# A message-passing layer on Trainium2: the normalised rows h in the second gather buffer and 13 further rows, the residual in pieces of three tiles

## The chip, the cores and the metric

The kernel runs on one core of one Trainium2 chip. The metric is the device time of one execution in microseconds (us), the median of several runs. Five engines work side by side, each through its own list of instructions in order: PE (TensorE, matmuls), DVE (VectorE), ACT (ScalarE), POOL (GpSimd), and SP (SyncE), which here only issues DMA transfers. They meet at semaphores: an instruction that waits for one holds everything behind it on its own engine.

## The reference

There are 6250 nodes with 96 features, and 206250 directed edges sorted by destination, each with 96 attributes.

```python
h = jnp.maximum(_layernorm(x, axis=-1), 0.0)
m = h[src] + edge_attr
aggr = jax.ops.segment_sum(m, dst, num_segments=6250)
hidden = jax.nn.relu(aggr @ W1 + b1)              # 96 -> 192
out = x + (1.0 + eps[0]) * h + hidden @ W2 + b2    # 192 -> 96
```

## The kernel before

**Blocks.** The nodes are cut into 49 blocks (NT) of 128. For 45 of them (NM) the sum of `h[src]` is made without a gather: DVE builds one-hot matrices of the sources' high and low parts (`z`, `lo_hot`, in four chunks a block, function `chunk`), PE multiplies them into counts of sources per destination (`octet`), ACT moves the counts to `adj`, and PE multiplies `adj` with h held in two fp16 parts (`sum_slots`). The edge attributes of a block are summed on PE by one-hots of the destinations (`sum_edges`, 72 matmuls).

**Gathered blocks.** The last four blocks (45 to 48, called gathered block 0 to 3) take the other way: SP loads their edge attributes, sources and destinations (`load_gathered`, 12 transfers), and POOL adds the rows h[src] onto the attributes in place with indirect DMAs from a copy of h in DRAM, 36 gathers of 128 rows for each block (line 524). Their sums are attached to the ordinary blocks 14, 24, 34 and 42 (ATTACHED). Two buffers are used in turn; each has GROUPS * GT = 36 rows of 96 values per partition, 72 rows together in `gather_home`. `gathered_buffer(j)` names the buffer of gathered block j.

**What else lies in these buffers.** At the start the raw `dst` and `src` lists (D and S) lie in the first and the second buffer. After that h itself (`h_sb`, 49 rows per partition) lies in `gather_home`: in all 36 rows of the first buffer and 13 of the second. h is read until the residual x + (1 + eps) h has been made in `x_sb` (function `residual`, line 734), which DVE does in pieces at the end of blocks 2 and later; `res_ready` counts them. Piece 0 is the 13 tiles 36 to 48, which frees the second buffer; six pieces of six tiles follow. So gathered block 0 goes into the second buffer, gathered block 1 into the first.

**Keys.** The packed (destination, source) keys of two blocks at a time come as a window from DRAM, fetched by POOL with an indirect DMA (`fetch`, line 486) that stands between the gathers in POOL's list: one fetch for every 23/3 gathers (FETCH_EVERY, FETCH_PER). Window 8 stands ahead of gather 31 (counted from 0 over all gathered blocks), window 9 ahead of gather 39, window 10 ahead of gather 46. Ahead of gather 36, the first of gathered block 1, POOL waits once for `gather_in` of that block's buffer (line 515), that is for its loads. Gathers are also held back to a pace of 13 per 3 blocks by `edges_done` (line 523). DVE takes window q in block 2(q - 1), between its first and second chunk (`pick`, line 676); PE and ACT then turn the keys for blocks 2q and 2q + 1.

**Order on DVE in a block b:** chunk 0; `pick` in even blocks; chunk 1; the one-hots of block b + 1's edges (`edge_hots`, which waits for that block's `dst` load, line 762); in blocks 14, 24, 34, 42 the one-hots of a gathered block; the output addition of block b - 4 (`finish`); the join of block b - 2's two partial sums (`next_join`, line 792); chunks 2 and 3; a residual piece. **On PE:** eight octets with the previous block's slots between them; after octet 2 come the turn of the joined sums (line 1090), the edge sum (line 1079) and the small layers.

**Order on SP.** For b from 3: wait for the edge sum of block b - 3 (`edges_done` at b - 2), then the eight loads of block b. Behind block 5's loads it issues gathered block 0's, behind block 12's those of gathered block 1, behind blocks 18 and 28 the other two (they wait for the sum that frees the buffer). Then the store of block b - 7.

Of the kernel before, what the change touches and what calls it, by code (L numbers as in the profile page):

```python
# [12 lines left out]
P = 128  # L13
# [8 lines left out]
GROUPS = P // GROUP  # L22
GT = 9
SPLIT = 100
TURN = 3
# [11 lines left out]
ATTACHED = (14, 24, 34, 42)  # L37
# [8 lines left out]
DEVIATION_AT = (15, 24)  # L46
RES_FIRST = 36
RES_ROWS = 6


def build(nc, x, src, dst, edge, w1, b1, w2, b2, eps, out):
    N, C = x.shape
    E = src.shape[0]
    H = w1.shape[1] // C
    NT = -(-N // P)
    NM = NT - GATHERED
# [4 lines left out]
    MPAIRS = -(-NM // 2)  # L61
    GE = P * GT
    ELAST = E - GE
    GCOLS = PAIRS * 2 * GROUPS
# [21 lines left out]
    with ExitStack() as ctx:  # L86
        def sb(name, shape, dt=F32):
            return ctx.enter_context(nc.sbuf_tensor(name, shape, dt))
# [16 lines left out]
        dst_sb = [sb(f"dst{k}", [P, GROUPS, GT], I32) for k in range(TURN)]  # L105
        gather_home = sb("gathered_edges", [P, 2, GROUPS, GT, C])
        gathered = [gather_home[:, k, :, :, :] for k in range(2)]
        gather_dst = [sb(f"gather_dst{k}", [P, GROUPS, GT], I32) for k in range(2)]
# [14 lines left out]

        h_sb = gather_home[:, :, :, :, :].rearrange("p k g t c -> p (k g t c)")[:, 0:NT * C].rearrange("p (t c) -> p t c", c=C)
        packed_lo = adj_home[:, :, :, :].rearrange("p k h n -> p (k h n)")[:, 0:4 * DW].rearrange("p (e four) -> p e four", four=4)[:, :, 2:4]
# [97 lines left out]
        words_ready = sem("words_ready")  # L223
# [101 lines left out]
        THIRDS = [slice(0, 16), slice(16, 32), slice(32, NT)]  # L325
        RES = [(RES_FIRST, NT)] + [(t, t + RES_ROWS) for t in range(0, RES_FIRST, RES_ROWS)]

# [12 lines left out]
        def gathered_buffer(j):  # L340
            return (j + 1) % 2

# [6 lines left out]
        def _(sp):  # L349
# [56 lines left out]
            for b in range(TURN, NM):  # L406
                sp.wait_ge(edges_done, b - TURN + 1)
                load(b)
                if b == TURN + 2:
                    sp.wait_ge(h_stored, 32)  # L410
                    sp.wait_ge(res_ready, 1)
                    load_gathered(0)
                if b == TURN + 2 + len(RES):
                    sp.wait_ge(res_ready, len(RES))
                    load_gathered(1)
                if attached(b - TURN - 1) is not None and attached(b - TURN - 1) + 2 < GATHERED:
                    j = attached(b - TURN - 1)
                    sp.wait_ge(gather_summed, j + 1)
                    load_gathered(j + 2)
                if b >= STORE_LAG:  # L420
                    store(b - STORE_LAG)
                if attached(b - STORE_LAG) is not None:
                    store_gathered(attached(b - STORE_LAG))
# [145 lines left out]
        def _(v):  # L569
# [206 lines left out]
            def finish(b):  # L776
                v.wait_ge(out_done, b + 1)
                if b < RES_FIRST:
                    v.wait_ge(res_ready, 2 + b // RES_ROWS)
                if b >= OBS:  # L780
                    v.wait_ge(out_stored[b % OBS], 16 * (b // OBS))
                nc.vector.tensor_tensor(ob[b % OBS][:, :], x_sb[:, b, :], mlp_ps[:, OUT_AT:OUT_AT + C], ALU.add).then_inc(out_ready, 1)  # L782
# [17 lines left out]
            def finish_gathered(j):  # L800
                v.wait_ge(gather_out_done, j + 1)
                if j >= 1:
                    v.wait_ge(gather_stored, 16 * j)
                nc.vector.tensor_tensor(gather_ob[:, :], x_sb[:, NM + j, :], mlp_ps[:, GATHERED_OUT_AT:GATHERED_OUT_AT + C], ALU.add).then_inc(gather_out_ready, 1)
# [473 lines left out]
```

## Time and profile before

| | before |
|---|---|
| median of 3 runs | 525.16 us (523.21 to 527.09) |
| the profiled execution | 525.82 us |
| its span, first to last instruction | 523.9 us |
| mean granted TensorE clock | 0.997 of full |
| PE, matmuls | 469.9 us (90%) |
| PEld, weight loads beside them | 446.9 us (85%) |
| DVE | 482.8 us (92%) |
| ACT | 414.3 us (79%) |
| POOL | 299.4 us (57%) |
| DMA | 110.03 MB, mean 210 GB/s |

The span is the traced part; the profiled execution's own time is 1.9 us longer. A share near 100% says that an engine is rarely idle, not that it decides the end at that moment: in stages the deciding engine differs, so the rows further down are taken by stretch and by queue. An "idle before" in square brackets is what the engine waited for just ahead of the instruction.

### The profile page before, as it was taken

The page shows a single profiled execution, that of the slowest core. Times are in us where ns is not written, and L with a number is a line of the kernel's source. Part 1 is how long each engine was busy: PE and PEld are TensorE (multiplying, and loading weights), DVE is VectorE, ACT ScalarE, POOL GpSimd, SP SyncE. Part 2 cuts the span into 40 slices and gives each one's busy share as a digit, 9 for nine tenths or more (in the row PEclk, how much of TensorE's full clock was granted, in tenths as well). Part 3 has the DMA queues.
Part 4 walks back from the last instruction along what each step waited for, and adds up shares of the span by engine and source line. Part 5 has one row for each costly group of instructions (what it writes and reads, how often), then busy time and mean ns, then how long its engine had stood idle before and what let it go on. Part 6 is the DMA issues. An engine that isn't in the chain of part 4 may idle for free.

```text
span 523.9 us, 22551 instructions
## 1 busy us (share of the span) xinstructions
PE 469.9 (90%) x9174; PEld 446.9 (85%) x9174; DVE 482.8 (92%) x727; ACT 414.3 (79%) x637; POOL 299.4 (57%) x188
## 2 busy tenths in 40 slices
PE   0525789999999999999999999999999999999994
PEld 0414688999899899999999999999999999998994
DVE  7998999999999999989999998899999999999870
ACT  0798777788888887888888788888888888886861
POOL 1330000788888888687888888888888881000000
PEclk9999999999999999999999999999999999999998
DMA  6769888998889987999998789999888887765000
GB/s 204 246 210 251 248 239 243 265 251 225 210 218 237 293 228 177 259 239 277 220 231 212 181 219 254 276 246 229 209 221 191 212 216 187 201 194 148 6 9 21
DMA packets 96867, 110.03 MB, mean 210 GB/s; under 512 B 68900, under 2 KB 70552, under 8 KB 96630
## 3 DMA queue, kind: packets, MB, share of 16 engines
q1 hardware_dynamic: 74854, 98.39, 63.1%
q0 software_dynamic: 21904, 10.13, 15.2%
q8 instruction: 75, 1.23, 0.9%
q14 instruction: 34, 0.28, 0.2%
HBM read 102.00 MB, written 6.48 MB: 207 GB/s over the span
## 4 chain that ended last, share of the span: by engine, by line
PE 77%; DVE 8%; SPq 6%; issue 4%; ACT 3%; DMA 1%; DVEq 0%; ACTq 0%
PE agg_ps L1085 31%; PE oct_ps L1073 22%; PE agg_ps L1079 14%; PE key_ps L1097 5%; PE mlp_ps L1102 4%; SPq L374 3%; DVE lo_hot L595 2%; ACT adj L917 2%; DVE z L595 1%; SPq L375 1%; SPq L373 1%; PE key_ps L1090 1%; DVE hot L602 1%; DMA gathered_edges<-in_dst 1%; ACT hid L930 1%
## 5 line engine op out<-in xcount | busy, mean ns | idle before, releaser
L917 ACT ACTIVATE adj<-oct_ps 128x784 f16<-128x784 f32 x360 | 299.5, 865 | 74.8 <-PE oct_ps L1073 70.6
L524 POOL DMA_INDIRECT gathered_edges<-h_rows,gather_src x144 | 264.5, 1837 | 48.6 <-issue 41.8
L1085 PE MATMUL agg_ps<-hl,adj 128*128 128x192 f16 x2205 | 232.9, 246 | 0.6 <-issue 0.3
L595 DVE TENSOR_TENSOR lo_hot<-iota_z,key 128x2048 f16<-128x2048 f16 x180 | 219.0, 1217 | 0.0
L1073 PE MATMUL oct_ps<-z,lo_hot 128*128 128x98 f16 x2880 | 190.7, 209 | 15.6 <-DVE lo_hot L595 7.8
L1073 PEld LDWEIGHTS oct_ps<-z,lo_hot 128*128 128x128 f16 x2880 | 164.3, 99 | 19.1 <-issue 8.2
L1085 PEld LDWEIGHTS agg_ps<-hl,adj 128*128 128x128 f16 x2205 | 173.5, 97 | 3.1 <-ACT adj L917 0.7
L595 DVE TENSOR_TENSOR z<-z_marks,key 128x1568 f16<-128x1568 f16 x180 | 173.9, 966 | 0.4 <-PE oct_ps L1073 0.4
L1079 PE MATMUL agg_ps<-edges,hot 128*32 128x96 f32 x3240 | 77.5, 250 | 2.3 <-DVE hot L748 2.3
L1079 PEld LDWEIGHTS agg_ps<-edges,hot 128*32 128x32 f32 x3240 | 68.0, 111 | 7.7 <-DVE hot L748 2.6
L486 POOL DMA_INDIRECT win<-packed_keys,row_i x23 | 26.8, 1166 | 68.4 <-DMA gathered_edges<-in_edge_attr 61.8
L980 ACT ACTIVATE hot<-hot 128x1152 f32<-128x1152 f16 x44 | 51.4, 1168 | 5.4 <-DVE hot L595 3.7
L595 DVE TENSOR_TENSOR hot<-iota_z,rel 128x1152 f16<-128x1152 f16 x44 | 33.3, 758 | 1.5
L1097 PE MATMUL key_ps<-aggT,w_sb 96*96 96x128 f32 x180 | 30.0, 288 | 2.4 <-issue 1.1
L930 ACT ACTIVATE hid<-key_ps,b_sb 96x128 f32<-96x128 f32 x90 | 27.3, 356 | 2.2 <-PE mlp_ps L1102 1.5
L1097 PEld LDWEIGHTS key_ps<-aggT,w_sb 96*96 96x96 f32 x180 | 21.0, 162 | 9.0 <-ACT key L905 3.2
L792 DVE TENSOR_REDUCE agg<-agg_ps 128x96 f32<-128x192 f32 x45 | 15.9, 353 | 12.9 <-PE agg_ps L1085 12.8
L1102 PE MATMUL mlp_ps<-w_sb,hid 97*128 97x96 f32 (+1 forms) x180 | 26.5, 269 | 0.7 <-ACT hid L930 0.7
L1102 PEld LDWEIGHTS mlp_ps<-w_sb,hid 97*128 97x128 f32 (+1 forms) x180 | 23.6, 191 | 0.9 <-ACT hid L930 0.9
L953 ACT ACTIVATE gathered_edges<-x_sb,shift,rstd 128x96 f32<-128x96 f32 x49 | 17.9, 452 | 0.5 <-DVE shift L619 0.5
L782 DVE TENSOR_TENSOR ob<-x_sb,mlp_ps 128x96 f32<-128x96 f32 x45 | 11.1, 247 | 6.9 <-PE mlp_ps L1102 6.9
L1090 PE MATMUL key_ps<-ident,agg 128*96 128x128 f32 x45 | 12.6, 280 | 5.3 <-DVE agg L792 3.9
(145 smaller groups left out, 186.3 us busy)
## 6 DMA issues: line engine op xcount, KB each, us to landing
edges<-in_edge_attr SPq DMA_DIRECT2D x180, 432.0 KB
gathered_edges<-in_edge_attr SPq DMA_DIRECT2D x16, 432.0 KB
dst<-in_dst SPq DMA_DIRECT2D x180, 4.5 KB
gathered_edges<-h_rows,gather_src POOLq DMA_INDIRECT x144
out<-ob SPq DMA_DIRECT2D x45, 48.0 KB
packed_keys<-adj SPq DMA_DIRECT2D x1, 1632.0 KB, 6.0
h_rows<-gathered_edges SPq DMA_DIRECT2D x1, 1200.0 KB, 9.2
h_rows<-gathered_edges SPq DMA_DIRECT2D x1, 1152.0 KB, 8.4
```

The source lines that it names most:

```text
L486: nc.gpsimd.indirect_dma_start(out=to[:, :, :].rearrange("p e two -> p (e two)"), out_offset=None, in_=keys_dram, in_offset=bass.IndirectO ...
L524: nc.gpsimd.indirect_dma_start(out=gathered[k][:, g, t, :], out_offset=None, in_=h_dram, in_offset=bass.IndirectOffsetOnAxis(ap=gather_src ...
L595: return nc.vector.tensor_tensor(out.rearrange("p t (w two) -> p t w two", two=2), marks[0:out.shape[0], 0:width].rearrange("p (o w two) - ...
L917: return nc.scalar.activation(adj[k][:, :, 2 * OCT * o:2 * OCT * (o + 1)].rearrange("p h (t q) -> p t h q", q=2), oct_ps[:, o % 2, :].rear ...
L930: last = nc.scalar.activation(to[0:C, j, :], key_ps[0:C, at + P * j:at + P * (j + 1)], ACT.Relu, bias=b1_sb[:, j:j + 1])
L953: last = nc.scalar.activation(h_sb[:, t, :], x_sb[:, t, :], ACT.Relu, bias=shift[:, t:t + 1], scale=rstd[:, t:t + 1])
L980: nc.scalar.activation(hot[b % 2][:, :, :], hot16[:, :, :], ACT.Copy).then_inc(hot_ready, 1)
L1073: last = nc.tensor.matmul(oct_ps[:, o % 2, P * t:P * t + ZW], lo_hot[o // 2][:, at, :], z[o // 2][:, at, :], start=True, stop=True)
L1079: last = nc.tensor.matmul(sums[GROUP * g:GROUP * (g + 1), :], hots[:, g * GT + t, :], rows[:, g, t, :], start=fresh and t == 0, stop=False ...
L1085: last = nc.tensor.matmul(agg_ps[buf][:, 0:2 * C], adj[buf][:, h, :], hl[:, h, :], start=False, stop=(h == NT - 1), skip_group_check=True)
L1097: last = nc.tensor.matmul(key_ps[0:C, at + P * j:at + P * (j + 1)], w1_sb[:, j, :], turned_sums[:, :], start=True, stop=True)
L1102: last = nc.tensor.matmul(mlp_ps[:, at:at + C], hidden_values[0:C + 1 - j, j, :], w2_sb[0:C + 1 - j, j, :], start=(j == 0), stop=(j == H - 1))
```

## The change

h moves to the second buffer and 13 rows appended behind it: `gather_home` grows from 72 to 85 rows (4992 bytes per partition more). Gathered blocks 0 and 2 now use the first buffer, 1 and 3 the second. Gathered block 0's load no longer waits for a residual piece or the stored h, only for the key words and steps made from D. The residual is cut into pieces of three tiles: twelve for tiles 0 to 35, which share the second buffer, then one for the four gathered tiles 45 to 48, then three for tiles 36 to 44. These are 16 pieces at the ends of blocks 2 to 17 (the change's one-line summary says 17). Gathered block 1's load is issued behind block 17's loads (5 + 12) and waits for the first twelve pieces. The output additions wait for their piece.

```diff
--- before.py
+++ after.py
@@ -44,8 +44,7 @@
 STORE_LAG = 7
 KEYS_AFTER = 24
 DEVIATION_AT = (15, 24)
-RES_FIRST = 36
-RES_ROWS = 6
+RES_ROWS = 3
 
 
 def build(nc, x, src, dst, edge, w1, b1, w2, b2, eps, out):
@@ -60,6 +59,8 @@
     PAIRS = -(-NT // 2)
     MPAIRS = -(-NM // 2)
     GE = P * GT
+    GATHER_ROWS = GROUPS * GT
+    assert NT >= GATHER_ROWS and GATHER_ROWS % RES_ROWS == 0
     ELAST = E - GE
     GCOLS = PAIRS * 2 * GROUPS
     SPLITS = GCOLS // SPLIT
@@ -103,8 +104,8 @@
         edge_home = sb("edges", [P, TURN, GROUPS, GT, C])
         edges = [edge_home[:, k, :, :, :] for k in range(TURN)]
         dst_sb = [sb(f"dst{k}", [P, GROUPS, GT], I32) for k in range(TURN)]
-        gather_home = sb("gathered_edges", [P, 2, GROUPS, GT, C])
-        gathered = [gather_home[:, k, :, :, :] for k in range(2)]
+        gather_home = sb("gathered_edges", [P, GATHER_ROWS + NT, C])
+        gathered = [gather_home[:, GATHER_ROWS * k:GATHER_ROWS * (k + 1), :].rearrange("p (g t) c -> p g t c", t=GT) for k in range(2)]
         gather_dst = [sb(f"gather_dst{k}", [P, GROUPS, GT], I32) for k in range(2)]
         gather_src = [sb(f"gather_src{k}", [P, GROUPS, GT], I32) for k in range(2)]
         z_home = sb("z", [P, CHUNKS, CHUNK, ZW], F16)
@@ -121,7 +122,7 @@
         keyT = [sb(f"keyT{k}", [P, P], F16) for k in range(2)]
         win_lo = [win[k][:, :, :].rearrange("p e two -> p (e two)").bitcast(F16).rearrange("p (e four) -> p e four", four=4)[:, :, 2] for k in range(WINS)]
 
-        h_sb = gather_home[:, :, :, :, :].rearrange("p k g t c -> p (k g t c)")[:, 0:NT * C].rearrange("p (t c) -> p t c", c=C)
+        h_sb = gather_home[:, GATHER_ROWS:GATHER_ROWS + NT, :]
         packed_lo = adj_home[:, :, :, :].rearrange("p k h n -> p (k h n)")[:, 0:4 * DW].rearrange("p (e four) -> p e four", four=4)[:, :, 2:4]
         packed = adj_home[:, :, :, :].rearrange("p k h n -> p (k h n)").bitcast(I32)[:, 0:2 * DW].rearrange("p (e two) -> p e two", two=2)
         scratch = [gathered[k].rearrange("p g t c -> p (g t c)").bitcast(I32) for k in range(2)]
@@ -323,7 +324,9 @@
 
         ROWS = [slice(0, HALF), slice(HALF, NT)]
         THIRDS = [slice(0, 16), slice(16, 32), slice(32, NT)]
-        RES = [(RES_FIRST, NT)] + [(t, t + RES_ROWS) for t in range(0, RES_FIRST, RES_ROWS)]
+        RES_SHARED = GATHER_ROWS // RES_ROWS
+        RES = [(t, t + RES_ROWS) for t in range(0, GATHER_ROWS, RES_ROWS)] + [(NM, NT)] + [(t, min(t + RES_ROWS, NM)) for t in range(GATHER_ROWS, NM, RES_ROWS)]
+        assert 2 + RES_SHARED < ATTACHED[0] + 3
 
         def all_stored(engine):
 
@@ -338,7 +341,7 @@
             return ATTACHED.index(b) if b in ATTACHED else None
 
         def gathered_buffer(j):
-            return (j + 1) % 2
+            return j % 2
 
         def edge_rows(b):
             return edges[b % TURN]
@@ -407,11 +410,12 @@
                 sp.wait_ge(edges_done, b - TURN + 1)
                 load(b)
                 if b == TURN + 2:
+                    sp.wait_ge(words_ready, 1)
+                    sp.wait_ge(steps_ready, 1)
+                    load_gathered(0)
+                if b == TURN + 2 + RES_SHARED:
                     sp.wait_ge(h_stored, 32)
-                    sp.wait_ge(res_ready, 1)
-                    load_gathered(0)
-                if b == TURN + 2 + len(RES):
-                    sp.wait_ge(res_ready, len(RES))
+                    sp.wait_ge(res_ready, RES_SHARED)
                     load_gathered(1)
                 if attached(b - TURN - 1) is not None and attached(b - TURN - 1) + 2 < GATHERED:
                     j = attached(b - TURN - 1)
@@ -775,8 +779,7 @@
 
             def finish(b):
                 v.wait_ge(out_done, b + 1)
-                if b < RES_FIRST:
-                    v.wait_ge(res_ready, 2 + b // RES_ROWS)
+                v.wait_ge(res_ready, b // RES_ROWS + (1 if b < GATHER_ROWS else 2))
                 if b >= OBS:
                     v.wait_ge(out_stored[b % OBS], 16 * (b // OBS))
                 nc.vector.tensor_tensor(ob[b % OBS][:, :], x_sb[:, b, :], mlp_ps[:, OUT_AT:OUT_AT + C], ALU.add).then_inc(out_ready, 1)
@@ -799,6 +802,7 @@
 
             def finish_gathered(j):
                 v.wait_ge(gather_out_done, j + 1)
+                v.wait_ge(res_ready, RES_SHARED + 1)
                 if j >= 1:
                     v.wait_ge(gather_stored, 16 * j)
                 nc.vector.tensor_tensor(gather_ob[:, :], x_sb[:, NM + j, :], mlp_ps[:, GATHERED_OUT_AT:GATHERED_OUT_AT + C], ALU.add).then_inc(gather_out_ready, 1)
```

## Rows read from the trace of the kernel before

**Rows 1.** Busy time in three stretches: PE, PEld, DVE, ACT, POOL, clock, DMA share, GB/s.
```profile
95.00:115.00 20.00, 19.64 (x384) 18.56 (x382) 19.93 (x27) 16.38 (x25) 17.26 (x10) 1.00 0.97 270
...
255.00:295.00 40.00, 39.82 (x793) 38.47 (x790) 39.36 (x53) 34.39 (x51) 34.21 (x20) 1.00 0.87 221
...
521.00:524.00 3.00, 0.00 (x0) 0.00 (x0) 0.00 (x0) 0.00 (x0) 0.00 (x0) 0.50 0.03 6
```
**Rows 2.** Chain of waits, the edge sums on PE: start us, us, piece.
```profile
101.15 1.62 PE agg_ps L1079 x72
...
193.90 3.11 PE agg_ps L1079 x144
...
215.87 1.62 PE agg_ps L1079 x72
...
226.21 1.62 PE agg_ps L1079 x72
...
236.07 1.62 PE agg_ps L1079 x72
```
**Rows 3.** DVE in order of time: start us, us, line, operation [idle before <-releaser].
```profile
27.76 0.28 DVE L676 TENSOR_SCALAR keyT<-win,base 128x128 f16<-128x128 int32 x1
...
99.31 0.23 DVE L762 TENSOR_TENSOR rel<-dst,gbase 128x72 f16<-128x72 int32 x1
...
171.48 0.23 DVE L762 TENSOR_TENSOR rel<-dst,gbase 128x72 f16<-128x72 int32 x1 [2.26 <-DMA dst<-in_dst]
...
190.58 0.22 DVE L762 TENSOR_TENSOR rel<-dst,gbase 128x72 f16<-128x72 int32 x1
...
193.18 0.35 DVE L792 TENSOR_REDUCE agg<-agg_ps 128x96 f32<-128x192 f32 x1
...
209.26 0.28 DVE L676 TENSOR_SCALAR keyT<-win,base 128x128 f16<-128x128 int32 x1
...
213.60 0.36 DVE L792 TENSOR_REDUCE agg<-agg_ps 128x96 f32<-128x192 f32 x1 [0.94 <-PE agg_ps L1085]
```
**Rows 4.** SP's DMA issues in order of time: start us, us, line.
```profile
74.64 0.34 SPq L374 DMA_DIRECT2D dst<-in_dst  x1
...
88.33 0.33 SPq L383 DMA_DIRECT2D gathered_edges<-in_edge_attr  x1
...
95.61 0.33 SPq L374 DMA_DIRECT2D dst<-in_dst  x1
...
167.75 0.33 SPq L374 DMA_DIRECT2D dst<-in_dst  x1
...
197.75 0.33 SPq L374 DMA_DIRECT2D dst<-in_dst  x1
```
**Rows 5.** POOL in order of time, key steps, window fetches, first gather of block 1.
```profile
17.04 2.90 POOL L496 TENSOR_TENSOR lo_hot<-gathered_edges 127x1632 int32<-127x1632 int32 x1 [13.95 <-DVE adj L643]
...
25.06 1.00 POOL L486 DMA_INDIRECT win<-packed_keys,row_i  x1 [0.30 <-issue]
...
93.21 1.09 POOL L486 DMA_INDIRECT win<-packed_keys,row_i  x1 [61.79 <-DMA gathered_edges<-in_edge_attr]
...
177.56 1.72 POOL L524 DMA_INDIRECT gathered_edges<-h_rows,gather_src  x1 [0.30 <-issue]
...
183.69 1.59 POOL L486 DMA_INDIRECT win<-packed_keys,row_i  x1 [0.31 <-issue]
...
201.31 1.18 POOL L486 DMA_INDIRECT win<-packed_keys,row_i  x1 [0.30 <-issue]
```
**Rows 6.** The residual line: durations in ns (min/median/max), start of first and last.
```profile
L734 DVE SCALAR_TENSOR_TENSOR x_sb<-gathered_edges,eps_sb,x_sb x7: 808/809/1509, 73.4 to 135.6; 128x576 f32<-128x576 f32 x6, 128x1248 f32<-128x1248 f32 x1
```
**Rows 7.** PE in order of time, before and after its clock rose.
```profile
40.53 3.11 PE L1079 MATMUL agg_ps<-edges,hot 128*32 128x96 f32 x72 [2.33 <-DVE hot L748]
...
47.78 1.49 PE L1073 MATMUL oct_ps<-z,lo_hot 128*128 128x98 f16 x16 [4.14 <-ACT key L905]
...
53.30 0.52 PE L1073 MATMUL oct_ps<-z,lo_hot 128*128 128x98 f16 x8
```

## Prediction

> **What bounds the kernel now.** I read the stretches first, then the chain of waits, then the queues of DVE, SP and POOL one after the other. In the stretch 95 to 115 us DVE is busy 19.93 of 20 us and PE 19.64; from 255 to 295 us PE is busy 39.82 of 40 us and DVE 39.36 [rows 1]. So DVE sets the pace early and PE sets it later, and neither has room: a stop of either goes nearly whole into the end. The chain gives the pace. Each block has one sum of its edges (72 matmuls); those of blocks 17 and 18 start 9.86 us apart, which is PE's own period, while blocks 5 to 14 take (193.90 - 101.15) / 9 = 10.31 us each [rows 2]. In DVE's rows the thing to see is where it stands: 2.26 us before the edge numbers of block 13, because a transfer was late, and nowhere at those of block 6 [rows 3]. SP's rows give how long it takes to issue one block's loads and one gathered block's; POOL's rows give the gathers, and between them the window fetches [rows 4, 5]. The last are what the argument hangs on. A window holds the packed keys of two blocks; DVE needs window q in block 2(q - 1), in order, ahead of its second chunk. Window 9 is fetched at 183.69 us and used at 209.26 us [rows 3, 5], so today it has 25 us to spare.
>
> **The change, part by part.** *h moves, buffer order swaps.* Gathered block 0 goes into the buffer that h has left; its load is still issued behind block 5's, where SP follows block 5's loads without a pause, and the first window fetch behind it waits for these very edges [rows 4, 5]. The two new waits there are for the key words and for the steps made from them, over at 17.04 + 2.90 = 19.9 us [rows 5]; the old one, the first residual piece, ended at 75 us and did not hold SP either [rows 6]: nothing gained or lost. The 13 further rows cost space, not time.
>
> *Residual.* A piece of 576 elements takes 0.809 us and one of 1248 takes 1.509 [rows 6]; that is 0.208 us plus 1.04 ns an element, so a piece of three tiles takes 0.51 and the one of four 0.61. Six and one pieces (6.36 us) become sixteen (8.24 us; the lines give 16, whatever the summary counts). Nine more instructions thus cost DVE 1.9 us in all. The Trainium skill, page "VectorE: DVE Perf Modes", section on the TRN2 errata, speaks against such a cut: a fixed cost is paid per instruction, so many small tiles pay it many times; the about 150 cycles that it gives would make this 1.4 us and the sum 0.5 us less. Where it falls matters more. Block 2 saves 1.0 us, blocks 3 and 4 save 0.3 each, but DVE then comes to block 6's edge numbers 1.6 us before 99.31. SP issues the last of these at 95.61 and is busy without a pause until then, so it can't be earlier; the one row that did wait for such a load started 171.48 - 167.75 = 3.7 us after its issue [rows 3, 4]. 95.61 + 3.7 = 99.3: I take the whole 1.6 us as given back (ends: all kept, all lost). From there blocks 5 to 8 save 4 x 0.30 = 1.2, blocks 9 to 13 pay 5 x 0.51 = 2.55, and the 2.26 us before block 13's numbers goes, because the twelve loads of gathered block 1 no longer stand ahead of them on SP. Sum: DVE is 0.9 us earlier at block 14. PE's own pace would bring it there at 101.15 + 9 x 9.86 = 189.9, before 193.0, so DVE still decides and the 0.9 us is real. The ends are -2.5 (the 1.6 kept) and +1.35 (the 2.26 stays).
>
> *The waits of the output additions* are on counts that DVE itself raised at least two blocks before, in its own order: nothing.
>
> *Gathered block 1's load, five blocks later.* This is the term that decides. SP now issues it behind block 17's loads, and these wait for the edge sum of block 14, which ended at 193.90 + 3.11 = 197.0 and will end at 196.1. Behind SP's wait nothing is late by itself: the store of block 10 goes out later by the issue of twelve loads, and its buffer is asked for four blocks on. But POOL waits for this load before gather 36, and behind that wait in POOL's order stand gathers 36 to 38 and then the fetch of window 9. Today POOL starts gather 36 at 177.56 without a stop. Step by step:
> - SP starts block 17's loads 0.75 us after the sum, at 196.85 (197.75 today) [rows 4].
> - Block 5's loads and the gathered load behind them took from 74.64 to the last edges' issue at 88.33, 13.7 us [rows 4]. So the last edges go out at 210.5.
> - POOL went on 93.21 - 88.33 = 4.88 us after that issue [rows 4, 5]: 215.4.
> - Three gathers took 183.69 - 177.56 = 6.13 us [rows 5]: window 9 is fetched at 221.5.
> - No view shows when a window lands. From below: the first one was used 27.76 - 25.06 = 2.70 us after its fetch began, with idle queues [rows 3, 5]. From above: the 4.88 us of the loaded queue. Block 18's loads and the next gathered load will be in the queues, so I take the loaded end: 226.4.
> - DVE stands at window 9 from about 209.4 (209.26 - 0.9 + two pieces of 0.51) to 226.4, 17 us.
>
> The Trainium skill, page "DMA: Bandwidth & Descriptors", section "Anatomy of one DMA", gives about 2.0 us plus size over 436 GB/s for a transfer issued from GpSimd; for a window of 128 KB this is an estimate of 2.3 us, and the sum by it would be 2.6 us less.
>
> *What of this reaches the end.* From the window to the point where DVE joins block 14's sums it takes 213.60 - 0.94 - 209.26 = 3.40 us without waiting, and PE starts the edge sum 193.90 - 193.18 = 0.72 us after a join begins [rows 2, 3]. So block 16's edge sum starts at 226.4 + 4.1 = 230.5 in place of 215.87: 14.6 us later. DVE's usual lead covers only the difference of 17 and 14.6. While DVE stands PE has nothing for some 14 us. Its clock then falls: with no matmul from 521 us on the granted clock is 0.50, the lower of the two levels, 1.2 GHz [rows 1], and before 53 us, after idle stretches, 72 edge matmuls took 3.11 us against 1.62 later [rows 2, 7]. Dense work began at 47.78 and the first rows at full rate are at 53.30 [rows 7], 5.5 us. About 1.8 us of this passes while PE waits for the join anyway; half of the other 3.7 is lost: 1.85 us (ends 0 and 2.75). After that PE runs on at its old periods (10.34 for block 17 [rows 2]) and DVE, which managed 10.31 with a 0.81 us piece in each block, keeps up. Gathered block 1 is then complete in time: ten gathers and a fetch took 201.31 - 177.56 = 23.75 us [rows 5], so 36 take 86 and end at 301, and block 24 asks for them at 226.21 + 7 x 9.86 + 16 = 311.
>
> **The sum:** -0.9 is inside the start of the chain; +14.6 + 1.85 = +16.5 us. The profiled execution took 525.82 us, so 542.3; that execution is 0.66 us above the median of the runs, so 541.7.
>
> **The rivals.** *The fetch is not held: not slower.* POOL would pass the wait before gather 36 in time and the window would land before about 213, when PE would first miss the chunk behind it. Then only the 0.9 to 2.5 us remain as gain: 525.16 - 0.9 = 524.3. It decides at the fetch: it would have to go out by 208, 13 us before the time worked out. Against it stands the order of SP's and POOL's instructions, and SP's 13.7 us behind a sum that ends at 196. For it: only that I misread which count POOL waits for.
>
> *A second stop at window 10.* From window 9's fetch to window 10's POOL needs 201.31 - 183.69 = 17.6 us [rows 5], and DVE comes to the second pick two blocks later, at least 19.7 us. If the gathers are slowed further by two gathered loads in neighbouring blocks, the 2 us of margin goes and each further us is lost whole, as DVE then has no lead; two or three us late give about 544.5. For it: gathered block 2's load follows one block behind. Against it: the 17.6 us were themselves measured under full queues.
>
> *A shorter stop.* If the load lands as fast as SP issues, the window in 2.7 us and the clock stays up, each of these at its low end: 14.6 - 1.6 - 2.2 = 10.8 us, 536.0.
>
> **How the numbers follow.** Forecast 0.86, second stop 0.05, shorter stop 0.05, not held 0.04. Terms at the low ends together give 536, at the high ends (late start +2.2, window and issue +1.5, clock +0.9) 546.3; they will hardly all meet, and the second stop lies inside: 536 to 546, widened by 0.5 below for the spread of runs. A difference under 1% can't be told from none here (the three runs span 0.7%); 1% is 530.4. Only the unheld fetch ends below that, inside 1%; a gain of over 1% would need the unheld fetch and more than the 2.5 us: 0.01.
>
> **What would show it.** DVE: one idle stretch of about 17 us before the key row of window 9 (line of the key transposition's input), put down to a transfer; no 2.26 us before block 13's numbers. POOL: idle from about 177 to 215 before gather 36. PE: some 14 us without work before block 16's edge sum, and a granted clock of 0.50 in it and shortly after. Edge sums of blocks 5 to 8 closer than 10.2 us apart, and blocks 18 on 9.86 apart. It is wrong if POOL's fetch of window 9 goes out before 208, or if DVE's stop is there but PE's is much shorter.

## The result, and the profile after

The changed kernel takes 546.61 us, median of 4 runs (545.26 to 548.5), against 526.12 us of the kernel before in the same comparison (4 runs, 523.21 to 529.8): a ratio of 1.0395, 95% interval 1.0357 to 1.0434. Medians and ratios here and below leave out executions over 1.5% above the fastest of the same kernel; there is one, 549.92 us, in the run called again. The profiled execution took 548.5 us, its span is 546.6 us and its mean granted clock 0.970 (before: 525.82, 523.9 and 0.997). The forecast, slower, named the main mechanism, but it was 4.9 us short, and the upper end of the range, 546.0, was 0.6 us too low.

From the page of the kernel after, the granted clock and DVE in 40 slices of 13.7 us; before, the clock had a 9 in every slice:

```profile
DVE  7997999899999957099999999999999989999970
PEclk9999999999999969669999999999999999999998
```

The holes lie in slices 15 to 18 (191 to 246 us). The stretches of the kernel after, columns as in [rows 1]:

```profile
95.00:115.00 20.00, 18.60 (x372) 17.71 (x371) 18.56 (x26) 15.67 (x23) 17.56 (x9) 1.00 0.92 246
197.00:204.00 7.00, 6.62 (x150) 6.37 (x151) 1.71 (x2) 1.16 (x1) 0.00 (x0) 0.55 0.01 2
218.00:232.00 14.00, 3.45 (x52) 2.99 (x49) 0.00 (x0) 3.67 (x5) 7.27 (x6) 0.70 0.87 245
255.00:295.00 40.00, 39.60 (x787) 38.17 (x785) 38.87 (x51) 34.11 (x51) 34.21 (x20) 1.00 0.88 212
```

The two middle stretches in the kernel before:

```profile
197.00:204.00 7.00, 7.00 (x105) 6.91 (x105) 6.75 (x10) 5.39 (x9) 5.78 (x4) 1.00 0.77 180
218.00:232.00 14.00, 14.00 (x259) 13.69 (x258) 13.27 (x18) 11.50 (x18) 11.86 (x8) 1.00 0.90 220
```

There are two holes, not one. From 218 to 232 us DVE does nothing: that one was forecast. From 197 to 204 PE is busy, but at a granted clock of 0.55, nearly all of it at the lower level, 1.2 GHz: that one was not. The edge sums in the chain of waits of the kernel after, as in [rows 2]:

```profile
101.12 1.62 PE agg_ps L1083 x72
...
180.93 1.67 PE agg_ps L1083 x72
197.38 6.02 PE agg_ps L1083 x144
...
237.47 3.04 PE agg_ps L1083 x72
...
249.24 1.62 PE agg_ps L1083 x72
259.11 1.62 PE agg_ps L1083 x72
```

Block 5 is where it was, blocks 5 to 13 are (180.93 - 101.12) / 8 = 9.98 us apart (10.24 before, where block 13's sum starts at 183.07), and the sum of block 14 comes 3.5 us later than before and takes 6.02 us in place of 3.11. The sum of block 17, at 249.24, is 23.0 us behind the 226.21 of [rows 2]; from there the period is 9.87 (9.86 before), and the execution ends 22.7 us later. PE's rows at the two holes, in order of time:

```profile
197.38 3.11 PE L1083 MATMUL agg_ps<-gathered_edges,hot 128*32 128x96 f32 x72 [4.89 <-DMA gathered_edges<-h_rows,gather_src]
200.24 3.13 PE L1083 MATMUL agg_ps<-edges,hot 128*32 128x96 f32 x72
...
235.66 0.83 PE L1077 MATMUL oct_ps<-z,lo_hot 128*128 128x98 f16 x8 [14.07 <-DVE lo_hot L599]
```

Before the first, PE waited 4.89 us for gathers of gathered block 0; before the second, 14.07 us for DVE. DVE's rows (those of [rows 3], lines moved by 3 or 4) show why:

```profile
189.19 0.21 DVE L766 TENSOR_TENSOR rel<-dst,gbase 128x72 f16<-128x72 int32 x1
...
191.77 0.35 DVE L795 TENSOR_REDUCE agg<-agg_ps 128x96 f32<-128x192 f32 x1
...
233.29 0.28 DVE L680 TENSOR_SCALAR keyT<-win,base 128x128 f16<-128x128 int32 x1 [17.16 <-DMA win<-packed_keys,row_i]
```

One stop of 17.16 us at window 9. SP's rows of block 17's first issue and of the last gathered edges, to set beside [rows 4]:

```profile
204.11 0.33 SPq L377 DMA_DIRECT2D dst<-in_dst  x1
...
218.96 0.33 SPq L386 DMA_DIRECT2D gathered_edges<-in_edge_attr  x1
```

And POOL's rows, as in [rows 5]:

```profile
94.12 4.62 POOL L490 DMA_INDIRECT win<-packed_keys,row_i  x1 [62.73 <-DMA gathered_edges<-in_edge_attr]
...
116.58 3.77 POOL L490 DMA_INDIRECT win<-packed_keys,row_i  x1 [0.30 <-issue]
...
127.76 3.21 POOL L528 DMA_INDIRECT gathered_edges<-h_rows,gather_src  x1 [0.30 <-issue]
...
156.48 3.77 POOL L490 DMA_INDIRECT win<-packed_keys,row_i  x1 [0.30 <-issue]
...
176.44 4.31 POOL L528 DMA_INDIRECT gathered_edges<-h_rows,gather_src  x1 [0.30 <-issue]
...
187.62 3.19 POOL L528 DMA_INDIRECT gathered_edges<-h_rows,gather_src  x1 [0.30 <-issue]
...
193.41 2.14 POOL L528 DMA_INDIRECT gathered_edges<-h_rows,gather_src  x1 [0.30 <-issue]
223.21 1.54 POOL L528 DMA_INDIRECT gathered_edges<-h_rows,gather_src  x1 [27.65 <-DMA gathered_edges<-in_edge_attr]
...
228.76 1.00 POOL L490 DMA_INDIRECT win<-packed_keys,row_i  x1 [0.30 <-issue]
```

Two things are to be seen. Gather 36 starts at 223.21 behind a wait of 27.65 us, and window 9 is fetched at 228.76 (183.69 in [rows 5]). And six rows ahead of these, three gathers and three fetches, take 3.19 to 4.62 us; in the kernel before no gather took over 2.44 and no fetch between 93 and 202 us over 1.59. So gathered block 0, which starts 0.9 us later than before, has its last gather begun only at 193.41, where before gather 36 was already out at 177.56. From the first fetch to the end of gather 35 it took 101.4 us in place of 84.1 for the same 41 rows. At the 1.75 us that a row took before, the six long rows make 12.4 us of these 17.4, the other 35 the rest.

The residual came out as worked out:

```profile
L738 DVE SCALAR_TENSOR_TENSOR x_sb<-gathered_edges,eps_sb,x_sb x16: 506/508/608, 73.6 to 251.3; 128x288 f32<-128x288 f32 x15, 128x384 f32<-128x384 f32 x1
```

### The profile page after: what moved, and what is told of

The parts are those of the page before. It is cut to its first block, busy times and chain, and to the rows that moved or that the text cites. A ratio compares the mean times of both kernels' runs of the same rounds, so it can differ in the third digit from the quotient of the medians.

```text
span 546.6 us, 22562 instructions
## 1 busy us (share of the span) xinstructions
PE 474.7 (87%) x9174; PEld 451.9 (83%) x9174; DVE 484.6 (89%) x736; ACT 414.1 (76%) x637; POOL 317.3 (58%) x188
## 4 chain that ended last, share of the span: by engine, by line
PE 75%; SPq 8%; DVE 4%; issue 4%; DMA 4%; POOL 3%; ACT 1%; DVEq 0%; ACTq 0%
PE agg_ps L1089 30%; PE oct_ps L1077 21%; PE agg_ps L1083 14%; PE key_ps L1101 5%; PE mlp_ps L1106 4%; SPq L377 3%; POOL gathered_edges L528 3%; SPq L376 2%; SPq L378 2%; PE key_ps L1094 1%; DVE hot L606 1%; ACT adj L921 1%; DVE lo_hot L599 1%; DMA win<-packed_keys,row_i 1%; DMA gathered_edges<-in_dst 1%
## 5 line engine op out<-in xcount | busy, mean ns | idle before, releaser
L528 POOL DMA_INDIRECT gathered_edges<-h_rows,gather_src x144 | 272.4, 1892 | 71.2 <-issue 42.7
L1083 PE MATMUL agg_ps<-edges,hot 128*32 128x96 f32 x3240 | 80.4, 255 | 2.3 <-DVE hot L752 2.3
L1083 PEld LDWEIGHTS agg_ps<-edges,hot 128*32 128x32 f32 x3240 | 70.7, 114 | 7.8 <-DVE hot L752 2.6
L490 POOL DMA_INDIRECT win<-packed_keys,row_i x23 | 36.8, 1601 | 69.3 <-DMA gathered_edges<-in_edge_attr 62.7
L795 DVE TENSOR_REDUCE agg<-agg_ps 128x96 f32<-128x192 f32 x45 | 16.0, 354 | 13.8 <-PE agg_ps L1089 13.7
L680 DVE TENSOR_SCALAR keyT<-win,base 128x128 f16<-128x128 int32 x23 | 7.4, 324 | 17.2 <-DMA win<-packed_keys,row_i 17.2
L1094 PE MATMUL key_ps<-ident,agg 128*96 128x128 f32 x45 | 12.9, 286 | 5.2 <-DVE agg L795 3.6
```

The costliest lines, as they stand in the source:

```text
L490: nc.gpsimd.indirect_dma_start(out=to[:, :, :].rearrange("p e two -> p (e two)"), out_offset=None, in_=keys_dram, in_offset=bass.IndirectO ...
L528: nc.gpsimd.indirect_dma_start(out=gathered[k][:, g, t, :], out_offset=None, in_=h_dram, in_offset=bass.IndirectOffsetOnAxis(ap=gather_src ...
L1083: last = nc.tensor.matmul(sums[GROUP * g:GROUP * (g + 1), :], hots[:, g * GT + t, :], rows[:, g, t, :], start=fresh and t == 0, stop=False ...
L1094: return nc.tensor.transpose(key_ps[0:C, TURN_AT:TURN_AT + P], agg[:, :], ident[:, :])
```

## The experiments

Two questions. **First:** is the loss the late load of gathered block 1 (it holds POOL, POOL holds the fetch, the fetch holds DVE), and not the extra pieces, the moved h or the swapped buffers? **Second:** what made the six rows long, and is it what put the result above the forecast? Rivals there: the short pieces themselves, the new place of h, or the place in DVE's order at which a POOL row starts.

**The load late, by itself.** In the kernel before:

```diff
-                if b == TURN + 2 + len(RES):
+                if b == TURN + 2 + 12:
```

> The kernel before, with one edit: gathered block 1's load is issued behind block 17's loads, not behind block 12's. Layout, buffer order and the pieces of six tiles stay. Theory 1 (the late load holds POOL and with it window 9): DVE stands 15 to 18 us for window 9, PE some 14, and as POOL's rows of gathered block 0 stay short, PE waits for nothing in block 14: edge sum 14 ends near 196, time 538 to 543, ratio 1.025 to 1.032. Rival (what costs is the new place of h or the new buffer order, not the load's time): no stop at window 9, within 1% of before.

541.03 us, ratio 1.025 (1.019 to 1.0311), with seven old pieces, h in its old place and the buffers unswapped. DVE's stop and PE's wait are there (the views of waits and of POOL in order of time):

```profile
DVE keyT L676 <- DMA win<-packed_keys,row_i: 18.2, 1, 18.2
```
```profile
216.80 1.54 POOL L524 DMA_INDIRECT gathered_edges<-h_rows,gather_src  x1 [38.75 <-DMA gathered_edges<-in_edge_attr]
```

PE stood 14.7 us, and its next edge sum took 3.04 us. No POOL row was long (over 2.7 us), and PE did not wait in block 14. This one line gives most of the loss.

**All but the late load and the short pieces.** In the kernel after, pieces of six tiles; the load then follows block 11, since it is tied to their number:

```diff
-RES_ROWS = 3
+RES_ROWS = 6
```

> The changed kernel with pieces of six tiles: nine pieces, and since the shared rows are then free after six, gathered block 1's load goes out behind block 11's loads. New layout and new buffer order stay. Theory 1: no stop at window 9, time within 1% of before (521 to 528). If the long POOL rows come from DVE's shorter piece of 0.51 us (theory 1a), none over 2.6 us in gathered block 0 and gather 35 starts near 175 to 178. If they come from the new place of the buffers (theory 1b), there are again some of 3 to 4.6 us, gather 35 starts later than 188, PE waits some us in block 14, and the time is 528 to 533.

525.79 us, ratio 0.9986 (0.9954 to 1.0017): no difference, and no stop. Moving h and swapping the buffers cost nothing that can be measured. With RES_ROWS = 4 the load goes out behind block 14:

> The changed kernel with pieces of four tiles: 13 pieces, gathered block 1's load behind block 14's loads. By the chain measured in the changed kernel (30.0 us from the edge sum that the load waits for to window 9 in place) window 9 is there near 203 to 205 us, DVE asks for it near 209: no stop, so theory 1 says within 1% of before (522 to 529), unless long POOL rows come with a piece of 0.61 us too; then gather 35 starts later than 185 and PE waits up to 5 us in block 14 (528 to 534). The rival, that any load later than block 12's costs, says 529 or more without a wait in block 14.

526.31 us, ratio 1.0014 (0.9978 to 1.0049). There was no stop at window 9 either, though its trace has four long rows and PE waited 3.3 us in block 14, where the sum then took 4.88 us in place of 3.11. The traced execution took 531.19 us; it is one of three at 530.2 to 531.3, while the other seven took 524.3 to 527.3. That is what such a wait would cost, 3.3 + 1.8 = 5.1 us; the other executions were not traced.

**The dose.** The kernel before, with the load behind block 16 (`TURN + 2 + 11`):

> The kernel before with gathered block 1's load behind block 16's loads, one block earlier than in the run late_only. By the measured chain window 9 is in place 30 us after the edge sum of block 13 ends (184.5): 214.5, some 5 us after DVE asks for it. DVE has a lead of 2.4 to 3.8 us there, so PE should lose only 1.5 to 3 us, and its idle stretch is too short to cost more at the lower clock: 526 to 529, ratio 1.002 to 1.008. If the cost is per block of delay (rival: about 3 us a block from 12 to 17), 537, ratio 1.02.

and with RES_ROWS = 3 in the old layout, which makes 13 pieces and puts the load behind block 18:

> The kernel before, with pieces of three tiles and nothing else: 13 pieces; the load of gathered block 1 goes out behind block 18's loads with them. Old layout and old buffer order. The runs so far had POOL rows over 3 us in gathered block 0 only with pieces of three tiles, but all of these in the new layout. Theory 1a (the short piece on DVE slows POOL): rows of 3.2 to 4.8 us in gathered block 0 here too, gather 35 starts at 186 to 195, PE waits 1 to 5 us for it in block 14; with a load one block later than in the changed kernel the stop at window 9 is 25 to 28 us, time 553 to 562. Theory 1b (it takes the new layout as well): none over 2.6 us, gather 35 starts near 177, time 549 to 553.

| load behind block | kernel | ratio (95%) | DVE's stop at window 9, us | PE's behind it, us |
|---|---|---|---|---|
| 14 | rows4 | 1.0014 (0.9978 to 1.0049) | none | none |
| 16 | late_16 | 1.0071 (1.0039 to 1.0104) | 7.1 | 3.6 |
| 17 | late_only | 1.025 (1.019 to 1.0311) | 18.2 | 14.7 |
| 18 | pieces_old | 1.0551 (1.051 to 1.0593) | 25.9 | 22.5 |

DVE's stop grows by 11.1 and then 7.7 us, about a block's period for a block; its lead over PE swallows some 3.5 us of it. So the price begins between blocks 14 and 16; block 15 was not run. The expectation for late_16 held PE's stop to be too short for the lower clock, and that was wrong: behind 3.6 us without work the granted clock was 0.50 (216.6 to 221.5 us). The chain of waits of late_16, from block 16's sum on:

```profile
218.41 3.04 PE agg_ps L1079 x72
230.26 1.62 PE agg_ps L1079 x72
```

The period from one to the other is 11.85 us in place of 10.34, 1.5 us lost to the clock, about as much as behind the 14 us (1.43).

**The fetches ahead of the wait.** In the kernel after, windows go out 15 gathers earlier from gather 36 on, so windows 9 and 10 stand ahead of POOL's wait:

```diff
+                ahead = 15 if j else 0
+                while j == 1 and (j * GROUPS * GT + ahead) * FETCH_PER >= (fetched - WINS - 1) * FETCH_EVERY:
+                    fetch(fetched)
+                    fetched += 1
...
-                        if ((j * GROUPS + g) * GT + t) * FETCH_PER >= ...
+                        if ((j * GROUPS + g) * GT + t + ahead) * FETCH_PER >= ...
```

> The changed kernel, with POOL's window fetches 15 gathers earlier from gather 36 on: windows 9 and 10 are fetched ahead of POOL's wait for gathered block 1's load. If the held fetch is the whole cost (theory 2), the stop of 17 us goes and the time is 528 to 533. If the late load costs by itself (theory 1), the stop moves: POOL starts gather 36 near 215 to 223 us as before, needs some 80 us for 36 gathers, so they end near 303 to 310, while PE asks for them in block 24 at 295 to 303: a wait of 5 to 12 us there with the low clock behind it, time 535 to 545.

538.59 us, ratio 1.0193 (1.0112 to 1.0274). DVE no longer waits for a window, but the time is mostly still lost. DVE's waits name the next late thing:

```profile
DVE rel L770 <- DMA dst<-in_dst: 12.1, 6, 7.9
```

These are edge numbers, the longest wait 7.9 us, at 245.42. SP's rows show where the delay lies: the loads of gathered blocks 1 and 2, 24 transfers, now stand one block apart, and block 19's edge numbers are issued behind both:

```profile
209.53 0.33 SPq L386 DMA_DIRECT2D gathered_edges<-in_edge_attr  x1
...
225.06 0.33 SPq L386 DMA_DIRECT2D gathered_edges<-in_edge_attr  x1
...
241.13 0.33 SPq L377 DMA_DIRECT2D dst<-in_dst  x1
```

PE then stood 6.9 us before block 18's sum at 247.38, which again took 3.04 us. The expectation had the time (535 to 545), but not the place: PE did not wait for gathers in block 24. It waited 2.4 us in block 14 too. So the fetch's place behind the wait is not the whole fault: once it is mended, a second late transfer takes part of its place.

**The kernel after again.** Three more comparisons of the unchanged kernel:

> The changed kernel once more, to see whether what set it 5 us over my forecast comes back. In its first trace DVE stood 17.16 us for window 9, as forecast, but edge sum 14 ended at 203.3 us and not at 196.1: PE waited 4.89 us for the gathers of gathered block 0, because six POOL rows of it took 3.2 to 4.6 us (before: none over 2.5). If these long rows belong to the kernel (theory 1), they come again at the same places, gather 35 starts later than 190 us and the ratio to before is 1.035 to 1.045. If they were an accident of that execution (theory 2), gather 35 starts near 177, PE does not wait in block 14 and the time is 538 to 543, ratio 1.025 to 1.033.

> The changed kernel as the yardstick for the next two on the same chip. Ratio to before 1.027 to 1.042, as in its two earlier sets; POOL rows over 3 us in gathered block 0 and a wait of PE in block 14 in its trace (theory: both are what my forecast lacked).

> The changed kernel once more, as the measure beside the next three. All theories: pieces spaced 9.98 us apart, two to six POOL rows of over 2.7 us between 93 and 195 us, DVE's stop at window 9 some 17 us, 540 to 547 us.

| | median us | ratio (95%) | rows over 2.7 us, 92 to 195 us | PE's wait in block 14, us | DVE's stop, us |
|---|---|---|---|---|---|
| after | 546.61 | 1.0395 (1.0357 to 1.0434) | 6 | 4.9 | 17.2 |
| again | 543.20 | 1.029 (1.020 to 1.038) | 5 | 2.4 | 17.7 |
| again2 | 541.31 | 1.028 (1.024 to 1.0319) | 2 | 0 | 17.0 |
| again3 | 541.31 | 1.0268 (1.021 to 1.0326) | 5 | 2.6 | 17.4 |

The stop is the same each time; the long rows and the wait in block 14 differ from execution to execution. So again fits neither theory of its expectation: the long rows came back, with a shorter wait. In again2's trace, against its expectation, the wait is missing, and the sum of block 16 starts at 229.02, forecast 230.5 (chain of waits):

```profile
229.02 2.99 PE agg_ps L1083 x72
240.59 1.62 PE agg_ps L1083 x72
```

The sum of block 17 starts at 249.24, 245.15, 240.59 and 243.75 us in the four traces, in the order of PE's wait and the sum of block 14 together (10.9, 8.1, 3.1 and 7.3 us). The traced executions took 548.5, 543.2, 541.45 and 542.3 us, so less than the differences of these sums reached the end. And again3, with a wait of 2.6 us in its trace, has the median of again2, which has none. That the wait makes the difference between medians of 541 and 547 is therefore not shown; one trace stands for four to six executions, and the repeats ran on three different chips.

**What makes rows long: piece length.** Six-tile pieces with the load kept behind block 17 (RES_ROWS = 6 and `TURN + 2 + 12` in the kernel after), and two three-tile pieces per block with the load behind block 11:

> The changed kernel with pieces of six tiles, gathered block 1's load still behind block 17's loads: from the changed kernel only the size of the pieces differs. If the pieces make the long POOL rows (theory 1a) there are none over 2.6 us in gathered block 0, PE does not wait for gathers in block 14, edge sum 14 ends near 196, DVE still stands 16 to 18 us for window 9, and the time is 2 to 7 us below again2: 538 to 543, ratio 1.024 to 1.032. If the new layout or the execution makes them (theory 1b), long rows and the wait are there, and the time is that of again2.

> The changed kernel with two pieces of three tiles, one behind the other, at the end of each block: 16 pieces over 8 blocks; gathered block 1's load behind block 11's loads. DVE's time for it in a block is then about that of a piece of six tiles (0.43 + 0.51), over as many blocks. If the length of DVE's block decides POOL's long rows (theory 1a), there are none over 2.6 us, gather 35 starts near 178, and the time is within 1% of before. If the single short instruction does it (theory 1c), there are rows over 3 us, gather 35 starts later than 185.

six_late: 542.59 us, ratio 1.0312 (1.027 to 1.0353), no faster than again2 on the same chip. One long row, no wait in block 14, DVE's stop 17.7. two_pieces: 527.95 us, ratio 1.0049 (1.0019 to 1.0079), so three-tile pieces with an early load cost about half a percent. Five long rows, a wait of 1.7 us in block 14, no stop. Up to here the long rows went with short pieces, nearly: none in before, late_only, late_16 and six_rows, one in six_late and in pieces_old, two to six in the others.

**The same kernel, gathered block 0 asked for two blocks later** (ATTACHED = (16, 24, 34, 42)):

> The changed kernel with gathered block 0's sum attached to block 16 in place of block 14, so that its gathers have two blocks more. What was missing in my forecast was, by theory 1, PE's wait for these gathers in block 14 and the low clock behind it: then that wait is gone though POOL's long rows stay, edge sum 14 ends at 192 to 196, DVE still stands 16 to 18 us for window 9, and the time is 4 to 8 us below again2, ratio 1.018 to 1.030. If the wait in block 14 cost nothing by itself (rival: the 5 us come from elsewhere), the time is within 2 us of again2.

542.22 us, ratio 1.0295 (1.0261 to 1.0329), beside again2's 541.31. Four long rows; DVE's stop was 15.25 us (16 to 18 expected). PE had no wait in block 14, but neither had again2's trace, so this does not price that wait: inconclusive.

**DVE's block length against piece length.** One more DVE instruction beside each piece, into a tile that nobody reads: 88 elements on the kernel after (pad and, once more, pad_b), 8 on six_late (six_plus).

```diff
+                nc.vector.scalar_tensor_tensor(pad[:, :], h_sb[:, 36, 0:88], eps_sb[:, 0:1], h_sb[:, 37, 0:88], ALU.mult, ALU.add)
                 nc.vector.scalar_tensor_tensor(x_sb[:, rows, :], h_sb[:, rows, :], eps_sb[:, 0:1], x_sb[:, rows, :],
```

> The changed kernel with one more DVE instruction of about 0.30 us beside each of its 16 residual pieces (it writes into a tile that nobody reads), so that a block takes DVE as long as with pieces of six tiles. Theory P (phase): how long a POOL row takes depends on where in DVE's order of one-hot instructions it starts; shorter pieces only shift POOL's rows against that order. Then the pieces are 10.25 to 10.31 us apart, at most one POOL row between 93 and 195 us takes over 2.7 us, gather 35 starts by 181, PE does not wait for it, and DVE's stop at window 9 stays at 17 to 18 us: 541 to 544 us. Theory S (the short pieces themselves): two to six such rows remain, gather 35 at 184 to 194.

> The same kernel as pad, for a second trace, as the number of long rows differs from trace to trace. P: again at most one long row. S: two to six.

> Pieces of six tiles with the load kept behind block 17, as in six_late (pieces 10.25 us apart, one long row), and one more DVE instruction of about 0.2 us beside each of the nine pieces, so that they are about 10.45 us apart, as in two_pieces (10.43 us, five long rows). P: the phases move again, and two or more POOL rows of over 2.7 us come back while the pieces run (94 to 160 us). S: none or one. The time says little: 541 to 545 in both.

pad: 554.18 us, ratio 1.0509 (1.0447 to 1.0571), pad_b 554.3 in one run; six_plus 539.83 in one run. The expectation for pad failed under both theories: the pieces were 10.3 us apart, as meant, but there were eight long rows in pad's trace and seven in pad_b's between 92 and 195 us, and up to 5.67 us long. Block length is therefore not what decides. But six_plus brought four long rows back with pieces of six tiles, as theory P expected, where none or one was expected if the short pieces were to blame: that theory falls too.

pad takes some 13 us more than again3. The added instructions are 16 x 0.30 = 4.8 us of DVE's time. The trace shows what else: the long rows hold back a fetch that stands ahead of POOL's wait, that of window 8 (188.89 us; 164.69 before), so DVE stands twice:

```profile
DVE keyT L681 <- DMA win<-packed_keys,row_i: 22.6, 4, 15.8
```

It stands 6.2 us at window 8 and 15.8 at window 9, and PE 5.6 and 12.9 us behind it.

What is left as a cause is in the repetition. POOL's rows in pad, and then in pad_b:

```profile
137.26 5.67 POOL L529 DMA_INDIRECT gathered_edges<-h_rows,gather_src  x1 [0.30 <-issue]
...
158.13 5.67 POOL L529 DMA_INDIRECT gathered_edges<-h_rows,gather_src  x1 [0.30 <-issue]
...
178.79 5.67 POOL L529 DMA_INDIRECT gathered_edges<-h_rows,gather_src  x1 [0.30 <-issue]
```
```profile
138.22 5.67 POOL L529 DMA_INDIRECT gathered_edges<-h_rows,gather_src  x1 [0.30 <-issue]
...
158.62 5.67 POOL L529 DMA_INDIRECT gathered_edges<-h_rows,gather_src  x1 [0.30 <-issue]
...
179.03 5.67 POOL L529 DMA_INDIRECT gathered_edges<-h_rows,gather_src  x1 [0.30 <-issue]
```

The same length to 0.01 us, six times in two executions. DVE in pad over the last of pad's three:

```profile
178.34 0.51 DVE L740 SCALAR_TENSOR_TENSOR x_sb<-gathered_edges,eps_sb,x_sb 128x288 f32<-128x288 f32 x1
178.77 0.97 DVE L600 TENSOR_TENSOR z<-z_marks,key 128x1568 f16<-128x1568 f16 x1
...
183.74 0.25 DVE L787 TENSOR_TENSOR ob<-x_sb,mlp_ps 128x96 f32<-128x96 f32 x1
183.91 0.35 DVE L797 TENSOR_REDUCE agg<-agg_ps 128x96 f32<-128x192 f32 x1
184.17 0.96 DVE L600 TENSOR_TENSOR z<-z_marks,key 128x1568 f16<-128x1568 f16 x1
```

The row starts 0.02 us into the first one-hot of a block and ends at 184.46, 0.29 us into the one-hot behind the join. The kernel after's 4.31 us row does the same (176.44 to 180.75; its one-hots follow one another without a break from 175.06, and the one behind the join starts at 180.47), and so does its 3.21 us row at 127.76. In this way 44 of the 64 long rows of all traces end at the output addition, at the join or in the first one-hot behind it. Of the others 8 end in the one-hots just behind a `pick`, 9 in or just behind a stop of DVE, and 3 in the second set of edge one-hots of block 14.

Over all 17 traces two conditions can be read. First, a piece: all 64 long rows end 3.4 to 6.7 us behind the start of a residual piece, that is in a block that DVE entered from one; from 280 us on, where no pieces are left, none of some 1,500 rows is long, and in two_pieces, whose last pieces start at 147.69, none that began behind 148.36. Second, a place: of 22 rows that began 0.25 to 0.50 us into the first `lo_hot` one-hot of an odd block behind a piece 21 were long, of 17 that began 0.69 to 0.98 us into it none; 17 that began 0.36 to 0.38 us into the same one-hot without a piece ahead took 2.25 or 2.26 us. Likewise all 15 rows that began in the first 0.03 us of the first `z` behind a piece were long, and none of 55 that began 0.13 to 0.26 us into it. But at the second chunk's `z` in even blocks behind a piece, 0.45 to 0.49 us in, only 9 of 37 were long, so a third condition is missing. The change spreads the pieces from blocks 2 to 8 over blocks 2 to 17: while gathered block 0 was gathered, ten blocks began behind a piece, five before. And it moves POOL's rows to other places. That would explain the counts, but it is read from the traces afterwards. The runs made for it show two things. pad, in both its traces, shows that DVE's instructions set POOL's long rows: one more of them beside each piece is all that it adds. And pad and six_plus exclude the block's length and the piece's length as the cause by themselves. Why DVE holds POOL there no run shows.

## Why the prediction came out as it did

**Right.** The chain from the sum of block 14 to window 9, link by link, after against forecast: 0.7 us to SP's first issue (0.75), 14.85 to the last gathered edges (13.7), 4.25 to POOL (4.88), 5.55 to the fetch (6.13), 4.53 to the keys (4.88). Together 29.9 us, forecast 30.3. For the last link the Trainium skill, page "DMA: Bandwidth & Descriptors", section "Anatomy of one DMA", has figures that gave an estimate of 2.3 us; the rows have 4.53, so the loaded end was the right choice, and the measurement decides. DVE's stop of 17.16 us (17), PE's of 14.07 (14), the way from the keys to block 16's sum, 4.18 us (4.1), the clock behind it, 11.77 - 10.34 = 1.43 us (1.85), and the absence of a second stop: all as put. late_only shows that the load alone does it, six_rows that h's place and the buffers cost nothing that can be measured.

**Right as well**, of the small terms: block 5 where it was (the 1.6 us given back), no 2.26 us before block 13's numbers, and the join of block 14 1.4 us earlier (0.9).

**The clock's term came near for a reason that its rows do not show.** The forecast took the rows from 40.53 us to just before 53.30 us [rows 7] for work at the lower clock. But the granted clock of the kernel before is 1.00 there (40 to 53.3 us), and why 72 edge matmuls took 3.11 us is open. That the lower clock nearly doubles them is shown by the kernel after: 3.13 us for the same 72 at 0.51 (197.4 to 203.4 us). That half of 3.7 us came near the measured 1.43 is in part luck.

**Wrong: the step "nothing gained or lost" on gathered block 0, and with it the start of the chain at 196.1.** The step looked at when the load goes out and not at the 41 POOL rows behind it, whose length I took as fixed; but they lengthen by what DVE does beside them, and the pieces, costed on DVE alone, had moved. So the wait of PE for these gathers stood in the sum at nothing. PE was at the sum at 197.38 - 4.89 = 192.5 (forecast 193.0), but stood 4.89 us for the gathers. Then the sum took 6.02 us at the lower clock, 2.9 more than its 3.11. The chain therefore began at 203.4, 7.3 us late. With -0.45 on the links, +0.1 behind the keys and -0.4 on the clock that makes +6.5; the sum of block 17 was 23.0 us late, forecast 16.5. Where the wait in block 14 is absent, in again2, the same sum is 240.59 - 226.21 = 14.4 us late. That its median of 541.31 meets the forecast's 541.7 is in part luck: the sum came 2.1 us earlier than forecast, and the rest of the traced execution, put at no change, took 1.25 us longer than before.

The range failed at the same step: its "late start +2.2" held DVE's terms and none for POOL. Before, POOL had some 12 to 15 us to spare: gather 35 starts at 175.24, the sums that waited for it came 3.2 to 6.2 us after its start, and block 14's sum is at 193.90. It was taken to keep them. Why one program gives 546.6 in one comparison and 541.3 in another stays open, and so does what sets the place at which POOL's rows first fall into DVE's order.

## What to carry to other kernels

Before a load is moved later, list what stands behind its waiter in that queue: here a window fetch three gathers behind POOL's wait stopped DVE for 17 us, and with the fetch moved ahead the next block's loads, behind the late transfers on SP, stopped it for 8. The price starts where the consumer's lead is used up (here between blocks 14 and 16) and then grows by about a block's period per block. When an edit changes the order or length of one engine's instructions, treat the row lengths of POOL's indirect DMAs as unknown again, and give them a term in the range: here it was PE's wait of up to 4.9 us and the lower clock behind it.

## What the runs showed of the hardware

**POOL's indirect DMA rows depend on DVE.** While DVE stood, gathers of 128 rows took 1.54 to 1.55 us and the fetch 1.00 (223.21 to 231.90 us in the kernel after); when it ran again, 2.13 (at 233.75), and beside dense one-hots up to 5.98 (two_pieces). The Trainium skill, page "DMA: Bandwidth & Descriptors", section "SWDGE vs HWDGE vs iDMA", says that GpSimd writes such descriptors into SBUF, from which DVE locks it out in a 2-port mode. The rows agree in that POOL is slower beside a busy DVE; in which mode DVE ran, and so whether this is the cause, no row shows.

**The clock falls after short waits.** After 3.6 us without work (late_16) the granted clock was 0.50, and the next 72 edge matmuls took 3.04 us in place of 1.62, the same as after 14 us. For gathered block 0 in block 14 PE waited 2.4 to 4.9 us in five traces, with another wait of 1.5 to 1.9 us shortly before; the sum of 144 matmuls behind it took 4.62 to 6.02 us in place of 3.11. After 1.7 us in two_pieces, with 0.2 before, the granted clock stayed at 1.00 and the sum took 3.18. So in this kernel a wait of 2.4 to 4.9 us there cost 1.5 to 2.9 us beyond itself.
